# A perceiver stack on one core: GpSimd takes part of a recurrence and of a scan's gates, a turning stage is cut, and three ends have fewer zero products

## The reference

```python
# L0_attn: attention in groups of 64 tokens, 16 heads of 16
q = rmsnorm(q, ln_w); k = rmsnorm(k, ln_w)
att = jnp.einsum('bghqd,bghkd->bghqk', q, k) * scale          # causal, then softmax
y = jnp.einsum('bghqk,bghkd->bghqd', att, v)
# L2_attn: a linear recurrence with complex diagonal, 128 states
Bu = jnp.einsum('hd,bld->blh', B_norm, x)
_, h = jax.lax.associative_scan(_binop, (Lam, Bu), axis=1)
y = jnp.einsum('oh,blh->blo', C, h).real + D * x
# L3_attn: a selective scan with 512 channels of 16 states
y = ys.transpose(1, 0, 2) + u * D_param
y = y * jax.nn.silu(x_gate)                                    # the gate
# L0_ffn, L1_ffn: routed experts
```

## Time and profile before

| | |
|---|---|
| median of 3 runs | 2923.56 us (2921.8 to 2924.08) |
| the profiled execution's own time | 2928.09 us |
| its span | 2926.3 us |
| TensorE busy | 94% of the span |
| VectorE, ScalarE, GpSimd busy | 50%, 34%, 5% |
| mean granted TensorE clock | 0.974 |

### The profile page before, as it was taken

The page is one execution under the profiler, slowest core; times in us unless marked ns, Lnnn a source line. Parts: engine busy times, 40 slices in busy tenths (PEclk is TensorE's granted clock), DMA queues, the critical chain, the costliest instruction groups (busy, mean ns, idle before and its releaser), DMA issues. The chain is left out here.

```text
span 2926.3 us, 46309 instructions
## 1 busy us (share of the span) xinstructions
PE 2739.0 (94%) x18078; PEld 1925.0 (66%) x18078; DVE 1463.5 (50%) x2504; ACT 991.5 (34%) x2207; POOL 151.5 (5%) x302
## 2 busy tenths in 40 slices
PE   8889979999998989799999988899999999999899
PEld 4676975666666569556666768746766654767545
DVE  3573225777777430354444461355445443999500
ACT  2342225666665213322222111232222224666200
POOL 2002021010100010100000010200000000000000
PEclk9989989999999989899999989999999999999999
DMA  9334863101111029321111025421111110222000
GB/s 294 100 129 149 297 216 79 45 30 45 30 30 47 1 98 327 138 71 52 65 61 49 33 112 213 161 84 56 66 57 52 55 38 2 80 72 73 33 1 15
DMA packets 96791, 259.99 MB, mean 89 GB/s; under 512 B 18916, under 2 KB 44232, under 8 KB 89048
## 3 DMA queue, kind: packets, MB, share of 16 engines
q1 hardware_dynamic: 85512, 240.17, 24.6%
q0 software_dynamic: 3840, 10.49, 1.1%
q10 hardware_dynamic: 7248, 6.65, 0.7%
HBM read 236.13 MB, written 21.14 MB: 88 GB/s over the span
## 5 line engine op out<-in xcount | busy, mean ns | idle before, releaser
L2206 DVE TENSOR_REDUCE buf<-acc 128x1 f32<-128x1024 f32 x128 | 150.8, 1220 | 346.0 <-PE acc L2098 346.0
L2175 ACT ACTIVATE buf<-acc,buf 128x1024 f32<-128x1024 f32 x128 | 142.7, 1115 | 343.9 <-DVE buf L2206 343.9
L2092 PE MATMUL acc<-buf 128*128 128x512 f32 x512 | 235.2, 602 | 5.7 <-ACT buf L2175 3.4
L359 PE MATMUL acc<-buf 128*128 128x256 f32 (+4 forms) x768 | 227.3, 491 | 11.2 <-PEq L89 11.2
L2120 PE MATMUL acc<-buf 128*128 128x256 f32 x1024 | 231.7, 379 | 1.5 <-ACT buf L2185 1.5
L2120 PEld LDWEIGHTS acc<-buf 128*128 128x128 f32 x1024 | 190.7, 190 | 25.7 <-issue 1.9
L359 PEld LDWEIGHTS acc<-buf 128*128 128x128 f32 (+2 forms) x768 | 133.3, 192 | 107.2 <-issue 98.7
L2222 DVE COPY buf<-acc 128x1024 f32<-128x1024 f32 x128 | 156.2, 1220 | 91.6 <-PE acc L2107 91.6
L2570 ACT ACTIVATE buf<-acc,buf 128x512 f32<-128x512 f32 x256 | 172.6, 686 | 75.1 <-DVE buf L2604 75.0
L2604 DVE TENSOR_REDUCE buf<-acc 128x1 f32<-128x512 f32 x256 | 159.0, 684 | 63.4 <-PE acc L2482 63.4
L2494 PEld LDWEIGHTS acc<-identity,buf 128*128 128x128 f32 x1024 | 114.3, 141 | 84.0 <-issue 78.2
(11 more groups left out here) (395 smaller groups left out, 4410.5 us busy)
## 6 DMA issues: line engine op xcount, KB each, us to landing
buf<-in_L_ffn_W SPq DMA_DIRECT2D x52, 1024.0 KB, 6.5
buf<-in_ctx SPq DMA_DIRECT2D x48, 768.0 KB, 4.8
buf<-in_ctxT SPq DMA_DIRECT2D x64, 512.0 KB, 5.5
buf<-in_L_ffn_w SPq DMA_DIRECT2D x36, 704.0 KB
buf<-state_rows SPq DMA_DIRECT2D x32, 512.0 KB
buf<-in_ctxT SPq DMA_DIRECT2D x96, 128.0 KB, 5.6
buf<-in_L_ffn_w SPq DMA_DIRECT2D x18, 640.0 KB
buf<-in_ctxT SPq DMA_DIRECT2D x32, 256.0 KB, 4.6
```

What stands on the lines that cost most here:

```text
L359: ins = pe.matmul(banks[n % nbanks][rows(r), 0:w], lhsT, rhs, start=(k == 0), stop=(k == len(pairs) - 1))
L2092: pe.matmul(acc_s[y][:, halves(h)], q0[:, b, 2 * r:2 * r + 2, :], ct0[x][:, halves(h)], start=True, stop=False)
L2175: act.activation(probs[u % 4][:, :], acc_s[u % 2][:, :], ACT.Exp, bias=negmax[:, u % 4:u % 4 + 1], accum_out=total[:, u % 4:u % 4 + 1]).th ...
L2206: dve.tensor_reduce(negmax[:, u % 4:u % 4 + 1], acc_s[u % 2][:, :], AX.X, ALU.max, negate=True).then_inc(max_ready, 1)
```

## The change

Five edits, in five functions.

1. load_tokens and routed_experts issue four zero products in place of six, at three ends in all (load_tokens, L0_ffn, L1_ffn).
2. In the recurrence GpSimd makes drive 1 and the first of the four turned states, in each half. The subtraction is released by DVE's fifth step (drive 0), the turned state by the sixth (the first scan). DVE's second scan waits for the subtraction, and TensorE for both turned_back and first_back.
3. Each of the 8 tiles has a bank of its own there, and the skipped products go ahead of the states' products: tiles 0 to 3 behind the wait for the weights, 4 and 5 when the first drives' banks are read, 6 and 7 when the second's are.
4. In the selective scan GpSimd multiplies chunks 0, 1 and 2 by their gates; DVE keeps chunk 3, and waits at its end for GpSimd's three.
5. The turning stage of the local attention handles six units. The queries of the second half of the sequences are transposed at its end into two banks that outlive it (late) and that the next stage also uses for its mixed values; ACT evicts them with eight instructions, four behind each of its first two exponents. The first mixing waits for these eight.

```diff
+            half = [P, B // 2, S]
+
+            TAKEN, ADDED, SCANNED, STEPS = 4, 5, 6, 10
+
+            def table(t):
...
+
+            def on_pool(pool):
+                for h in range(2):
+                    pool.wait_ge(steps, STEPS * h + ADDED)
+                    pool.tensor_tensor(drive[1][:, :], part[2][:, :], part[3][:, :], ALU.subtract).then_inc(subtracted, 1)
+                    pool.wait_ge(steps, STEPS * h + SCANNED)
+                    pool.tensor_tensor(by_batch(back[0][:, halves(h)]), by_batch(state[0][:, halves(h)]), table(ph.cos),
+                                       ALU.mult).then_inc(first_back, 1)
 
...
@@ -534,25 +554,36 @@
...
-                    if j >= 4:
-                        pe.wait_ge(added, j - 3)
+
+                def skipped(j):
+                    for k in range(DC):
+                        pe.matmul(out[j][:, tile(k)], xnT[:, k, tile(j)], Dd[:, k, :], start=(k == 0), stop=False)
+
+                def states(j):
                     for n, C in enumerate((Cre, Cre, Cim, Cim)):
-                        pe.matmul(out[j % 4][:, 0:D], back[n][:, tile(j)], C[:, :], start=(n == 0), stop=False)
-                    for k in range(DC):
-                        ins = pe.matmul(out[j % 4][:, tile(k)], xnT[:, k, tile(j)], Dd[:, k, :], start=False,
-                                        stop=(k == DC - 1))
+                        ins = pe.matmul(out[j][:, 0:D], back[n][:, tile(j)], C[:, :], start=False, stop=(n == 3))
                     ins.then_inc(read_out, 1)
+
+                for j in range(4):
+                    skipped(j)
+                pe.wait_ge(steps, TAKEN)
+                for j in (4, 5):
+                    skipped(j)
+                pe.wait_ge(turned_back, 1)
+                pe.wait_ge(first_back, 1)
+                for j in range(4):
+                    states(j)
+                pe.wait_ge(steps, STEPS + TAKEN)
+                for j in (6, 7):
+                    skipped(j)
+                pe.wait_ge(turned_back, 2)
+                pe.wait_ge(first_back, 2)
+                for j in range(4, NT):
+                    states(j)
                 pe.wait_ge(added, 5)
 
             def on_dve(dve):
                 c = Chain(dve, steps)
...
@@ -566,20 +597,20 @@
...
                     dve.wait_ge(act_steps, 1)
                     for n in range(2):
+                        if n == 1:
+                            dve.wait_ge(subtracted, h + 1)
                         c.link(dve.tensor_tensor_scan(state[n][:, halves(h)], decay[:, halves(h)], drive[n][:, :], 0.0,
                                                       ALU.mult, ALU.add))
                     g, f = state[0][:, halves(h)], state[1][:, halves(h)]
-                    c.link(times(back[0][:, halves(h)], g, ph.cos))
                     c.link(times(back[1][:, halves(h)], f, ph.minus_sin))
                     c.link(times(back[2][:, halves(h)], f, ph.minus_cos))
                     c.link(times(back[3][:, halves(h)], g, ph.minus_sin))
                     dve.sem_inc(turned_back, 1)
                 for j in range(NT):
                     dve.wait_ge(read_out, j + 1)
                     dve.wait_ge(added, j + 1)
                     statistics.tile(dve, j)
 
...
@@ -1253,7 +1284,7 @@
...
-                idle_products(chip, pe, acc_down[0], 6)
+                idle_products(chip, pe, acc_down[0], 4)
...
@@ -2010,7 +2041,7 @@
...
-            idle_products(chip, pe, spare, 6)
+            idle_products(chip, pe, spare, 4)
...
@@ -3014,10 +3045,6 @@
...
-                    for y in range(2):
-                        c = 2 * g + y
-                        dve.wait_ge(kept, c + 1)
-                        dve.tensor_tensor(u[:, c, :], u[:, c, :], gate[:, c, :], ALU.mult)
...
@@ -3027,6 +3054,16 @@
...
                 keep(1)
+                dve.wait_ge(kept, C)
+                dve.tensor_tensor(u[:, C - 1, :], u[:, C - 1, :], gate[:, C - 1, :], ALU.mult)
+                dve.wait_ge(gated, C - 1)
+
+
+            @block.gpsimd
+            def _(pool):
+                for c in range(C - 1):
+                    pool.wait_ge(kept, c + 1)
+                    pool.tensor_tensor(u[:, c, :], u[:, c, :], gate[:, c, :], ALU.mult).then_inc(gated, 1)
 
         jobs = []
...
@@ -3110,11 +3148,17 @@
...
+
+
+            for c in range(DC):
+                chip.names += 1
+                late.append(es.enter_context(nc.psum_tensor(f"acc{chip.names}", [P, HALF], F32)))
             with Stage(chip) as st:
-                banks = [st.psum(P, HALF) for _ in range(8)]
+                banks = [st.psum(P, HALF) for _ in range(6)]
                 turned = st.sem()
                 block = st.block()
-                units = [(n, c, h) for n in range(2) for c in range(DC) for h in range(2)]
+
+                units = [(0, 0, 0), (0, 1, 0), (1, 0, 0), (1, 1, 0), (1, 0, 1), (1, 1, 1)]
...
@@ -3126,6 +3170,9 @@
...
+                    for c in range(DC):
+                        for q in range(4):
+                            pe.transpose(late[c][:, tile(q)], qk[0][:, 4 + q, tile(c)], ident[:, :])
...
@@ -3160,11 +3207,11 @@
...
-            acc_m = [st.psum(P, HALF) for _ in range(2)]
+            acc_m = late
...
@@ -3222,6 +3269,8 @@
...
+                    else:
+                        pe.wait_ge(late_kept, 4 * DC)
...
@@ -3277,6 +3326,11 @@
...
 
+                def keep_late(c):
+                    for t in range(4):
+                        act.activation(a[:, 8:16, c, t // 2, t % 2, :], late[c][:, :].rearrange("p (b s) -> p b s", s=S),
+                                       ACT.Copy, scale=side[:, c, t:t + 1]).then_inc(late_kept, 1)
...
@@ -3286,6 +3340,8 @@
...
+                    if i < DC:
+                        keep_late(i)
                 statistics.root(act)
 
```

More of the change, by code:

```diff
@@ L225, in _ @@
                 work["sync"](sync)
+        if "pool" in work:
+            @block.gpsimd
+            def _(pool):
+                work["pool"](pool)
         @block.vector
@@ L522, in recurrence @@
         def recurrence(st, turned, banks, dve_copied, act_copied, act_steps, statistics):
-            driven, steps, turned_back, read_out, added = st.sems(5)
-            out = [turned[n % 2][n // 2] for n in range(4)]
+            driven, steps, turned_back, read_out, added, subtracted, first_back = st.sems(7)
+            out = [turned[n % 2][n // 2] for n in range(4)] + list(banks)
+            half = [P, B // 2, S]
+            TAKEN, ADDED, SCANNED, STEPS = 4, 5, 6, 10
+            def table(t):
+                return t[:, 0:S].unsqueeze(1).broadcast_to(half)
+            def on_pool(pool):
[5 more added lines that the diff above has]
+                                       ALU.mult).then_inc(first_back, 1)
             def on_pe(pe):
@@ L551, in on_dve @@
                 c = Chain(dve, steps)
-                half = [P, B // 2, S]
-                def table(t):
-                    return t[:, 0:S].unsqueeze(1).broadcast_to(half)
                 def times(to, value, t):
@@ L581, in on_dve @@
                     dve.wait_ge(read_out, j + 1)
-                    dve.tensor_tensor(X[:, j, :], X[:, j, :], out[j % 4][:, 0:D], ALU.add).then_inc(added, 1)
+                    dve.tensor_tensor(X[:, j, :], X[:, j, :], out[j][:, 0:D], ALU.add).then_inc(added, 1)
                     dve.wait_ge(added, j + 1)
@@ L590, in on_sync @@
                 chip.wait_far(sync)
-            return {"pe": on_pe, "dve": on_dve, "sync": on_sync}
+            return {"pe": on_pe, "dve": on_dve, "sync": on_sync, "pool": on_pool}
         normed_jobs(chip, X, xn, xnT, ident, [],
@@ L2921, in selective_scan @@
             rows_in = st.sems(2)
-            diag_ready, exp_done, driven, scanned, out_ready, summed, kept = st.sems(7)
+            diag_ready, exp_done, driven, scanned, out_ready, summed, kept, gated = st.sems(8)
             block = st.block()
@@ L3058, in local_attention @@
         twice, causal = sb(P, P), sb(P, 8, S)
+        late = []
         with ExitStack() as inner:
@@ L3166, in local_attention @@
             (scored, max_ready, shifted, exp_done, summed, inverted, normed, turned, turned_copied, mixed, mixed_copied,
-             y_filled, added) = st.sems(13)
+             y_filled, added, late_kept) = st.sems(14)
             statistics = Statistics(chip, st, X)
```

4 lines of the change are left out of this document (removed).

## The result

| | before | changed |
|---|---|---|
| median of 7 runs | 2923.56 us (2921.8 to 2927.72) | 2916.68 us (2909.92 to 2918.47) |
| profiled execution: own time, span | 2928.09, 2926.3 | 2917.6, 2915.8 |
| mean granted clock | 0.974 | 0.977 |

What follows compares the result with a forecast made beforehand. TensorE, busy 94% of the span, was taken to bound the kernel. Ends -1.3, recurrence +0.4, gates -1.2 and local attention -5 summed to -7.1, from the median 2923.56 to 2916.5 us; range 2908.5 to 2922.5.

Steps and rivals of the forecast that it cites:

- Local attention, -5: Local attention: turning stage 2.6 us shorter, and first scores at full clock behind a shorter pause; -5 us.
- the gain of 7.2: Local attention: second shift at 158.4 if the first scores run at full clock behind the shorter pause; -7.2 us.
- Its rival, that the clock doesn't follow: Local attention: clock stays 0.50 at the first scores, only the stage's -2.6 remains; 2918.9 us in all, 16%.
- Recurrence, +0.4: Recurrence: GpSimd and DVE wait for each other, TensorE pauses before the last tiles and pays half clock; +0.4 us.
- taking turns: GpSimd and DVE, both with two SBUF operands: one waits for the other's whole operation; 2916.5 us in all, 50%.
- The pause of 3.4: Recurrence: TensorE waits 3.4 us, until 1718.2, for the second half's turned states.
- the 2.3 that I had charged: Recurrence: TensorE's loss at half clock behind its pause before the last tiles; 2.3 us.
- The lower bound that I gave for it, -1.9: Recurrence: TensorE at full clock ends at 1724.4 instead of 1726.33; -1.9 us.
- Gates, -1.2: Selective scan's gates: DVE's product waits for GpSimd's second gate; -0.9 us in the middle, -0.3 at the end, sum -1.2.
- Ends, -1.3: Three ends with four zero products: next stages open sooner, some transposes at half clock; -1.3 us, bounds -3.9 and +2.0.
- My slower rival: Three ends: clock rises late, transposes and first products at half clock, +5.0 us; attention's clock stays 0.50; 2925.2 us, 9%.
- Side by side: Recurrence and scan's gates: GpSimd and DVE work without waits, -4.4 and -3.4 us; -14.1 in all, 2909.5 us, 25%.

Runs made afterwards that it cites:

- experiment 7: The kernel before with eight products of zeros added behind the 32 transposes of the local attention's turning stage, nothing shortened; ratio 0.9987, -3.8 us.
- experiment 8: The kernel before plus a stage where DVE and GpSimd run 128x512 operations alone and together; with two SBUF operands each, a pair costs 1.66 us.
- experiment 4: The kernel before with only the four zero products in place of six at the three ends; ratio 1.0013, 3.8 us slower.

## Why the prediction was right, point by point

The predicted time, 2916.5, was met by 0.2 us, but part of that is luck. By the ratio the change is -10.2 (7.3 to 13.2), and the forecast of -7.1 lies just outside that. Term by term:

- **Local attention, -5**: the steps of the mechanism held, the stage at -2.6 and the clock behind a pause of 1.83, with the fall ahead of the first turn. I discounted the gain of 7.2 to 5 for what might come back; nothing did. Alone it measured -6.7, and experiment 7 shows the clock's part. Its rival, that the clock doesn't follow, is out.
- **Recurrence, +0.4**: taking turns is shown, by the stretched operations and by experiment 8, and the prices were near (GpSimd 1.26 for the 1.2 that I took). Four things were off. A turn costs less than the whole other operation (+0.65 and +1.3 for the turned states, not +1.0 and +2.0). The states' products take 1.79 a tile, not 1.56. The pause of 3.4 came out at 0.51: the skipped products began only when the last weights had landed, 12.9 behind the opening, and ran mostly at half clock, in time that was free; so the states' products began at 17.0 and not at 15.5, and the 2.3 that I had charged for a half clock behind the pause was not paid. And I had TensorE end the stage, where DVE's adds do. The stage gained about 1.4. The lower bound that I gave for it, -1.9, was the nearer one.
- **Gates, -1.2**: -0.95 in the middle, and -0.47 at the end for the -0.3 that I had, by the steps as written.
- **Ends, -1.3**: this step failed in its sign, by the ratio of experiment 4 (+3.8). The openings came nearly as priced (DVE idles 1.03, 0.72 and 0.58 at them in the changed kernel, 3.6 less than before in sum, for at most 3.9), and the transposes were at half clock at one of three ends, behind load_tokens (3.3 to 3.6 in all three traces with four products there). At the ends themselves that sums to -1.4 in experiment 4's trace, as forecast. What I had no term for is the second cross attention, 3.5 longer in three of the four traces with four products at L0_ffn, and in one of ten with six; why is open. My slower rival had the ends' cost nearly right (+5.0) by another mechanism: it wanted the rise over 1.5 us behind the last transpose at each end, and no end shows that; behind load_tokens the products lost 0.27, so the rise came about 0.5 into them (estimate from 7.40 against 7.13).
- **Side by side** fell: -14 would have needed GpSimd's work for free. The one thing said for it was thin: of GpSimd's 32 sums of 616 ns, three stood beside a DVE copy from PSUM and the others beside nothing.

So by the single ratios an attention term 1.7 too small and a recurrence term 1.8 too dear stood against the ends' 5 us too cheap; the parts alone sum to -1.5 by ratios and to -7.7 by medians, and the whole to -7 or -10. That the sum was met is not evidence for each term.

## What to carry to other kernels

Before work is given to GpSimd, look at what VectorE runs beside it: in these traces a VectorE operation with one operand in PSUM cost nothing, and one with all operands in SBUF made one of the two wait; holding the GpSimd operation until a scan with a PSUM operand starts gave the time back (1.4 us). A short stretch of products that keeps TensorE busy over a pause can be worth as much as a shorter stage, and cutting such products can cost more than they take (behind load_tokens 0.6 was gained and 2.3 paid). Stages in which nothing is changed differ by 1 to 5 us from one trace to the next, and the one that opens at 34.15 before takes 73.8 to 84.7 us in the fourteen traces. So a part is judged by its own stage over several traces with the clock at the same place, and by ratios of many runs; and parts that share one set of runs of before share its error.

## What the runs showed that I had not expected

- DVE's tensor_scalar of 128x512 within SBUF, 0.43 us alone, takes 1.37 beside GpSimd.
- GpSimd and DVE in turns cost 1.66 us a pair, where the two alone are 1.26 and 0.69.
- A stage of 481 us is 3 to 5 us longer in 4 of 14 traces, those in which the stage ahead of it opened under 0.4 or 1.5 us behind the clock's rise (bounds drawn after the fact).
